# Attention with a mixture of experts on one core: the first two token tiles of an expert as one pair, and the order of the second layers

## The chip, the cores and the metric

The kernel runs on one core of one Trainium2 chip. The metric is the device time of the whole program in microseconds, lower is better. A time is the median of several runs. Besides the runs there is one profiled execution, from which all rows below come.

Names of the engines in the rows: PE is TensorE (matmuls), PEld its loads of the stationary operand, DVE is VectorE, ACT is ScalarE, POOL is GpSimd, SP is SyncE. A q behind a name is that engine's instruction queue.

## The reference

The input is 2 x 1024 tokens of 512 values. They are normalized, and three things are added to the input: a causal attention (16 heads in 4 groups), a shared feed-forward layer, and a mixture of 32 experts of which each token uses six.

```python
def _route(xf, Wr, br):
    s = jax.nn.sigmoid(xf @ Wr.T + br)
    ...
    idx = jax.lax.top_k(masked, K)[1]          # K = 6 of E = 32
    ...
    return (idx, w * SCALE)
...
def step(acc, ew):
    w1, w2, g = ew
    h = jnp.square(jax.nn.relu(xf @ w1.T)) @ w2.T     # 512 -> 256 -> 512
    return (acc + g[:, None] * h, None)
...
shared = jnp.square(jax.nn.relu(hidden_tensor @ Ws1.T)) @ Ws2.T
return shared + moe_out
...
x = x + _L0_attn_ref(xn, ...) + _L0_ffn_ref(xn, ...)
```

## The kernel before

All products are of float32 values split into an upper part (fp32r) and a lower part (the rest), and made of three matmuls: upper x upper, upper x lower, lower x upper. ScalarE writes the upper part by a copy, VectorE the lower part by a subtraction.

Stages: normalizing, routing and the shared layer up to about 136 us; then the experts; then the attention, to the end. In routing VectorE makes the tables `tile_hot` (MAXT wide, line 1526) from which TensorE makes the list of tokens (line 761), and a transfer fills the padding of the expert outputs with zeros (`act.dma_start(y_d[MINT * P:, :])`, line 1183).

The experts' work is cut into tiles of 128 tokens. An expert has the tiles `lo` to `hi`, from a table that is computed in the run (`count_tiles`; at least two for each expert). With these inputs there are 111 tiles, 3 to 5 for an expert, and 20 of the 32 experts have 3. GpSimd gathers the token rows of a tile into one of four slots of `xg`. For each tile TensorE runs:

- `hidden_tile` (line 855): 12 matmuls of 256 columns with the tokens stationary and the first-layer weights moving, into `ps_h`; then four turns (transposes) of the next tile's tokens (`transpose_gathered`, line 849) into `ps_x`;
- `output_tile` of the tile before (line 878): 6 matmuls of 512 columns into `ps_y`;
- `transpose_hidden` (line 890): two turns of the squares `mhsq` into `ps_g`.

Around these ScalarE does `relu_hidden`, the upper part of the next tokens (`upper_tokens`), the copy of the output (`copy_output`) and the upper part of the turned squares (`upper_hidden`); VectorE squares (`square_hidden`) and does the lower parts (`lower_tokens`, `lower_hidden`). SyncE stores the copied output.

The weights of an expert (1 MB) are loaded into one of two buffers `eraw`, three experts ahead, by `store_tiles` (line 487) at the start of its round for an expert. They are split in four pieces: `upper_weights` on ScalarE, `lower_weights` on VectorE, two experts ahead. Pieces 0 and 1 stand in the work of the expert's first tile, 2 and 3 after its last tile.

The order on each engine is the order of the code in `expert_tiles` (TensorE), `expert_uppers` (ScalarE) and `expert_lowers` (VectorE); every engine runs its own queue in order and waits on semaphores. The four experts of a round are written out (`s` is 0 to 3), and the tiles after the first are a loop on each engine.

## Time and profile before

| | us |
|---|---|
| runs, median of 3 | 1525.64 (1524.73 to 1525.66) |
| profiled execution, its own time | 1526.73 |
| span of its core | 1525.0 |
| TensorE busy with matmuls | 1509.9 (99%) |
| TensorE busy with weight loads | 1302.1 (85%) |
| VectorE busy | 1132.8 (74%) |
| ScalarE busy | 837.9 (55%) |
| GpSimd busy | 298.3 (20%) |

The mean granted clock of TensorE is 0.999 of its full speed. Matmuls overlap in the pipeline, so that their durations are longer than their spacing: the busy time says that TensorE has work, and the chain that ended last gives the spacing. Of that chain 96% of the span is TensorE's, 2% VectorE's and 1% transfers.

### The profile page before, as it was taken

What the parts mean: (1) busy time and instruction counts of PE and PEld (TensorE: products, weight loads), DVE (VectorE), ACT (ScalarE), POOL (GpSimd) and SP (SyncE); (2) the same over time, 40 slices, a digit from 0 to 9 for tenths busy, and PEclk for the clock granted to TensorE, in tenths of its full rate; (3) what the DMA queues carried; (4) which work ended last, traced back from release to release, by engine and by line L of the source; (5) the groups of instructions that cost most, each with busy time, mean ns of one, the idle gap of its engine ahead of it and who ended that gap; (6) DMA issues with size and microseconds to landing.
All of it is one profiled execution on the core that took longest, in us unless ns stands there. A gap on an engine that the chain in (4) does not pass through costs nothing.

```text
span 1525.0 us, 31150 instructions
## 1 busy us (share of the span) xinstructions
PE 1509.9 (99%) x8552; PEld 1302.1 (85%) x8553; DVE 1132.8 (74%) x2586; ACT 837.9 (55%) x1753; POOL 298.3 (20%) x540
## 2 busy tenths in 40 slices
PE   9998999999999999999999999999999999999998
PEld 8877998899899888888888888888888888888886
DVE  7896666666666669859949948967975994994896
ACT  5574666666666635535625635644553553553553
POOL 0003344334344311011002002102102101200211
PEclk9999999999999999999999999999999999999999
DMA  8874777777876612102102103422211210210111
GB/s 318 301 302 165 218 243 233 229 234 228 258 234 207 228 35 70 43 21 76 55 7 79 45 28 120 149 62 85 67 34 41 69 41 21 76 34 28 56 42 55
DMA packets 64774, 184.34 MB, mean 121 GB/s; under 512 B 7136, under 2 KB 7264, under 8 KB 60000
## 3 DMA queue, kind: packets, MB, share of 16 engines
q1 hardware_dynamic: 39888, 112.56, 21.1%
q0 software_dynamic: 16640, 54.54, 13.1%
q10 hardware_dynamic: 8208, 16.78, 2.8%
q8 instruction: 19, 0.31, 0.1%
q14 instruction: 19, 0.16, 0.0%
HBM read 123.29 MB, written 60.56 MB: 121 GB/s over the span
## 4 chain that ended last, share of the span: by engine, by line
PE 96%; DVE 2%; DMA 1%; issue 0%; ACT 0%; ACTq 0%; DVEq 0%; SPq 0%
PE bank L663 8%; PE bank L665 8%; PE bank L993 8%; PE bank L664 8%; PE ps_s L663 7%; PE ps_s L665 7%; PE ps_s L664 7%; PE ps_s L980 5%; PE ps_s L982 5%; PE ps_s L981 4%; PE ps_s L860 4%; PE ps_s L883 4%; PE ps_s L864 3%; PE ps_s L861 3%; PE ps_s L887 3%; PE ps_s L884 3%
## 5 line engine op out<-in xcount | busy, mean ns | idle before, releaser
L1322 ACT ACTIVATE probs<-probs,negmax 128x128 f32<-128x128 f32 (+7 forms) x256 | 197.4, 774 | 122.5 <-DVE negmax L1736 121.9
L1330 ACT ACTIVATE pT_hi<-bank 128x512 fp32r<-128x512 f32 x288 | 164.5, 595 | 143.4 <-PE bank L993 117.5
L1347 DVE TENSOR_TENSOR pT_lo<-bank,pT_hi 128x512 fp32r<-128x512 f32 x288 | 189.7, 684 | 41.0 <-ACT pT_hi L1330 40.0
L1736 DVE CUSTOM_DVE_ANT_0 probs<-ps_s,causal 128x128 f32<-128x128 f32 (+7 forms) x256 | 189.5, 753 | 17.1 <-PE ps_s L982 14.9
L427 POOL TENSOR_TENSOR settled<-ident 128x1 f32<-128x1 f32 x192 | 46.5, 242 | 788.7 <-DVE acc L1765 778.7
L993 PE MATMUL bank<-ident,probs 128*128 128x128 f32 x1152 | 157.0, 272 | 0.0
L993 PEld LDWEIGHTS bank<-ident,probs 128*128 128x128 f32 x1152 | 136.9, 141 | 19.8
L663 PE MATMUL ps_s<-xT_hi,wa_hi 128*128 128x512 f32 x384 | 152.7, 398 | 0.0
L665 PE MATMUL ps_s<-xT_hi,wa_lo 128*128 128x512 f32 x384 | 150.9, 393 | 0.0
L664 PE MATMUL ps_s<-xT_lo,wa_hi 128*128 128x512 f32 x384 | 150.2, 391 | 0.0
L1745 DVE TENSOR_SCALAR probs<-probs,rnorm 128x128 f32<-128x128 f32 (+7 forms) x256 | 133.4, 521 | 9.1
L980 PE MATMUL ps_s<-kT_hi,qT_hi 128*128 128x512 f32 (+5 forms) x384 | 134.0, 349 | 1.0 <-DVE qT_lo L1716 0.5
L982 PE MATMUL ps_s<-kT_hi,qT_lo 128*128 128x512 f32 (+5 forms) x384 | 131.2, 342 | 0.0
L981 PE MATMUL ps_s<-kT_lo,qT_hi 128*128 128x512 f32 (+5 forms) x384 | 130.9, 341 | 0.0
L663 PE MATMUL bank<-pT_hi,v_hi 128*128 128x512 f32 x288 | 123.6, 429 | 0.6 <-DVE cT_lo L1347 0.6
L623 POOL DMA_INDIRECT xg<-normed_tokens,comb_idx x112 | 111.8, 998 | 23.3 <-issue 18.1
L1347 DVE TENSOR_TENSOR hT_lo<-ps_s,hT_hi 128x256 fp32r<-128x256 f32 x111 | 47.2, 425 | 92.0 <-ACT hT_hi L1245 53.5
L665 PE MATMUL bank<-pT_hi,v_lo 128*128 128x512 f32 x288 | 113.5, 394 | 0.0
L1251 ACT ACTIVATE ysb<-ps_s 128x512 f32 x111 | 66.5, 599 | 84.9 <-PE ps_s L887 65.7
L664 PE MATMUL bank<-pT_lo,v_hi 128*128 128x512 f32 x288 | 112.7, 391 | 0.0
L652 POOL DMA_INDIRECT comb<-expert_outputs,comb_idx x96 | 105.2, 1096 | 19.6 <-issue 11.5
L663 PE MATMUL bank<-wa_hi,cT_hi 128*128 128x512 f32 x256 | 101.5, 396 | 1.4 <-DVE cT_lo L1347 1.4
(197 smaller groups left out, 3596.3 us busy)
## 6 DMA issues: line engine op xcount, KB each, us to landing
eraw<-we SPq DMA_DIRECT2D x37, 1024.0 KB
expert_outputs<-ysb SPq DMA_DIRECT2D x111, 256.0 KB
araw<-wa SPq DMA_DIRECT2D x37, 512.0 KB, 4.3
expert_outputs<-comb ACTq DMA_DIRECT2D x1, 16384.0 KB, 47.4
normed_tokens<-xn SPq DMA_DIRECT2D x4, 1024.0 KB, 10.0
out<-acc SPq DMA_DIRECT2D x16, 256.0 KB
acc<-x SPq DMA_DIRECT2D x2, 1024.0 KB, 13.8
turned_tokens<-xT_hi SPq DMA_DIRECT2D x2, 1024.0 KB, 7.6
```

The source lines that it names most:

```text
L663: pe.matmul(out_, lh, rh, start=(first and k == 0), stop=False)
L664: pe.matmul(out_, lh, rl, start=False, stop=False)
L665: mm = pe.matmul(out_, ll, rh, start=False, stop=(last and k == parts - 1))
L980: pe.matmul(o, q_h, kT_hi[:, ks], start=True, stop=False)
L981: pe.matmul(o, q_h, kT_lo[:, ks], start=False, stop=False)
L982: mm = pe.matmul(o, q_l, kT_hi[:, ks], start=False, stop=True)
L993: mm = pe.transpose(ps_t[blk % 2][:, h * P:(h + 1) * P], probs[:, i % 2, h, a * P:(a + 1) * P], ident[:, :])
L1322: act.activation(pr, pr, ACT.Exp, bias=negmax[:, i % 2, a:a + 1], scale=-1.0, accum_out=rowsum[:, i % 2, a:a + 1]).then_inc(exp_ready, 1)
L1330: act.activation(pT_hi[:, blk % RING, :], ps_t[blk % 2][:, :], ACT.Copy).then_inc(pt_hi_ready, 1)
L1347: dve.tensor_tensor(out_, whole, upper.bitcast(F32), ALU.subtract).then_inc(signal, 1)
L1736: dve.tensor_tensor_reduce(halves(probs[:, i % 2, a, 0:keys]), ps_s[:, s:s + parts, 0:keys // parts], halves(causal[:, SQ - keys:]), -1.0, ...
L1745: dve.tensor_scalar(pr, pr, rnorm[:, i % 2, a:a + 1], None, ALU.mult).then_inc(probs_ready, 1)
```

## The change

The change is in the experts' stage.

- `hidden_pair`: the first two tiles of each expert are one pair. The first-layer weights are stationary and 256 tokens move, so the hidden layer comes out turned, in two halves of 128 hidden values (`ps_p[0]`, `ps_p[1]`). Relu, Square, upper and lower part are made for each half (`relu_pair`, `upper_pair`, `square_pair`, `lower_pair`), without turns. ScalarE makes the upper part from the Relu with its own Square, VectorE squares for the lower part.
- `output_first`: the second layer of the pair's first tile goes half by half. The pair's second tile is done in the loop or ahead of the next pair.
- Tiles from the third on are done as before, in the loop, but the turns of their squares (`transpose_hidden`) now stand between the upper and the lower matmuls of the second layer of the tile before.
- The last tile's second layer stands whole ahead of the next expert's pair, in a bank of its own (`ps_y2`), and the turns of the next pair's second tile of tokens ahead of that (`ps_x2`).
- The four weight pieces stand one behind the other around the pair's steps; none is left for after the loop.
- Every expert gets at least three tiles (`LEAST`), and the bound MAXT goes from 160 to 177. With it the width of `tile_hot` and of the list matmuls grows, and the zero fill goes from 64 to 81 tiles.
- VectorE waits for `room_free` ahead of the attention's first maximum.

```diff
 MINT = T * TOPK // P
-MAXT = MINT + 2 * E
+LEAST = 3
+MAXT = max(LEAST * (E - n) + min(n * TILES, (T * TOPK + (P - 1) * n) // P) for n in range(E + 1))
...
+            def hidden_pair(lo, s):
+
+                w_hi, w_lo = w1(hi_slot(s)), w1(lo_slot(s))
+                both = lambda x, k: x[:, k, :, :].rearrange("p t n -> p (t n)")
+                for m in range(KM):
+                    ms = slice(m * P, (m + 1) * P)
+                    if m == 0:
+                        pe.wait_ge(mx_hi, lo + 2)
+                    for k in range(KD):
+                        pe.matmul(ps_p[m], w_hi[:, k, ms], both(xgT_hi, k), start=(k == 0), stop=False)
+                        pe.matmul(ps_p[m], w_lo[:, k, ms], both(xgT_hi, k), start=False, stop=False)
+                    if m == 0:
+                        pe.wait_ge(mx_lo, lo + 2)
+                    for k in range(KD):
+                        mm = pe.matmul(ps_p[m], w_hi[:, k, ms], both(xgT_lo, k), start=False, stop=(k == KD - 1))
+                    mm.then_inc(mh_ready, 1)
+
+            def output_first(lo, s):
+
+                w_hi, w_lo = w2(hi_slot(slot_of(s))), w2(lo_slot(slot_of(s)))
+                for m in range(KM):
+                    pe.wait_ge(mhhi_ready, past(lo + (m + 1)))
+                    pe.matmul(ps_y, hT_hi[:, s % 2, m, 0, :], w_hi[:, m, :], start=(m == 0), stop=False)
+                    pe.matmul(ps_y, hT_hi[:, s % 2, m, 0, :], w_lo[:, m, :], start=False, stop=False)
+                    pe.wait_ge(mhlo_ready, past(lo + (m + 1)))
+                    mm = pe.matmul(ps_y, hT_lo[:, s % 2, m, 0, :], w_hi[:, m, :], start=False, stop=(m == KM - 1))
+                mm.then_inc(my_ready, 1)
...
             def expert_tiles(e, s, lo, hi, es):
 
-                pe.wait_ge(ew_lo, (e + NSH) * WP + 2)
-                hidden_tile(lo, slot_of(s))
-                after = pair_bound(pe, e + 2)
+                turn_tokens(lo + 1, ps_x2)
                 if s:
-                    output_tile(lo - 1, slot_of(s - 1))
+                    output_upper(lo - 1, s - 1, ps_y2)
+                    output_lower(lo - 1, s - 1, ps_y2)
...
-                transpose_hidden(lo, (e + (NSH + 1)) * WP)
-                with pe.Fori(lo + 1, hi) as p:
+                after = pair_bound(pe, e + 2)
+                pe.wait_ge(ew_lo, (e + NSH) * WP + 2)
+                hidden_pair(lo, slot_of(s))
+                pe.sem_inc(mt_ready, 2)
+                turn_tokens(lo + 2, ps_x)
+                pe.wait_ge(ew_lo, (e + (NSH + 1)) * WP)
+                output_first(lo, s)
+                with pe.Fori(lo + 2, hi) as p:
                     hidden_tile(p, slot_of(s))
-                    output_tile(p - 1, slot_of(s))
+                    pe.wait_ge(y_copied, past(p - 1))
+                    output_upper(p - 1, s, ps_y)
                     transpose_hidden(p)
+                    output_lower(p - 1, s, ps_y)
                 return after
...
+            def upper_pair(lo, m, s):
+
+                act.wait_ge(mrelu_ready, past(lo + (m + 1)))
+                act.activation(hT_hi[:, s % 2, m, :, :].rearrange("p t n -> p (t n)"), prelu[:, m, :],
+                               ACT.Square).then_inc(mhhi_ready, 1)
...
             def expert_lowers(e, s, lo, hi, es):
                 slot = slot_of(s + 2)
-                square_hidden(lo)
-                lower_tokens(lo + 1)
+                if s:
+                    lower_tokens(lo + 1, 1)
...
                 lower_weights(e + 2, 0, slot)
-                lower_hidden(lo)
                 after = pair_bound(dve, e + 2)
                 lower_weights(e + 2, 1, slot)
-                with dve.Fori(lo + 1, hi) as p:
+                square_pair(lo, 0)
+                lower_pair(lo, 0, s)
+                lower_weights(e + 2, 2, slot)
+                square_pair(lo, 1)
+                lower_pair(lo, 1, s)
+                lower_tokens(lo + 2)
+                lower_weights(e + 2, 3, slot)
+                with dve.Fori(lo + 2, hi) as p:
                     square_hidden(p)
                     lower_tokens(p + 1)
-                    lower_hidden(p)
-                lower_weights(e + 2, 2, slot)
-                lower_weights(e + 2, 3, slot)
+                    lower_hidden(p, s)
```

On ScalarE, at an expert's start, the row read before from the third and fourth weight piece of the expert before (here `w_hi`) to the second piece of the next:

```order
L1235 ACTIVATE w_hi<-eraw 128x512 x2
L1239 REGISTER_ALU
L1241 ACTIVATE mrelu<-ps_s 128x256
L1229 REGISTER_ALU
L1230 ACTIVATE xgT_hi<-ps_s 128x512
L1234 ISA
L1235 ACTIVATE w_hi<-eraw 128x512
L1251 ISA
L1251 ACTIVATE ysb<-ps_s 128x512
L1245 ACTIVATE hT_hi<-ps_s 128x256
```

Now, from the second piece on (`prelu` is the pair's Relu, one half in each instruction):

```order
L1283 ACTIVATE w_hi<-eraw 128x512
L1295 ACTIVATE prelu<-bank 128x256
L1299 REGISTER_ALU
L1300 ACTIVATE hT_hi<-prelu 128x256
L1283 ACTIVATE w_hi<-eraw 128x512
L1295 ACTIVATE prelu<-bank 128x256
L1299 REGISTER_ALU
L1300 ACTIVATE hT_hi<-prelu 128x256
L1276 REGISTER_ALU
L1277 ACTIVATE xgT_hi<-ps_s 128x4x128
```

The third piece moved from behind the loop to between the two halves of the pair, and the copy of turned squares is gone for the pair.

On VectorE at the same place, before, with the first two pieces around the first tile's steps:

```order
L1653 TENSOR_TENSOR mhsq<-mrelu 128x256
L1347 TENSOR_TENSOR xgT_lo<-ps_s,xgT_hi 128x512
L1660 ISA
L1347 TENSOR_TENSOR w_lo<-eraw,w_hi 128x512
L1347 TENSOR_TENSOR hT_lo<-ps_s,hT_hi 128x256
```

and now, from the second piece on (`phsq` are the pair's squares):

```order
L1416 TENSOR_TENSOR w_lo<-eraw,w_hi 128x512
L1722 REGISTER_ALU
L1723 TENSOR_TENSOR phsq<-prelu 128x256
L1416 TENSOR_TENSOR hT_lo<-phsq,hT_hi 128x256
L1744 REGISTER_ALU
L1416 TENSOR_TENSOR w_lo<-eraw,w_hi 128x512
L1722 REGISTER_ALU
L1723 TENSOR_TENSOR phsq<-prelu 128x256
L1416 TENSOR_TENSOR hT_lo<-phsq,hT_hi 128x256
L1416 TENSOR_TENSOR xgT_lo<-ps_s,xgT_hi 128x4x128
```

The third piece's lower part moved to ahead of the second half's square.

On TensorE, in the loop over an expert's later tiles, before:

```order
L883 MATMUL ps_s<-wa_hi,hT_hi 128x512
L884 MATMUL ps_s<-wa_lo,hT_hi 128x512
L887 MATMUL ps_s<-wa_hi,hT_lo 128x512 x2
L891 REGISTER_ALU
L896 MATMUL ps_s<-ident,mhsq 128x128 x2
```

and now:

```order
L920 MATMUL ps_s<-wa_hi,hT_hi 128x512
L921 MATMUL ps_s<-wa_lo,hT_hi 128x512
L932 REGISTER_ALU
L934 MATMUL ps_s<-ident,mhsq 128x128 x2
L928 MATMUL ps_s<-wa_hi,hT_lo 128x512 x2
```

The two lower matmuls moved from ahead of the turns of the squares to behind them.

## Rows read from the trace of the kernel before

**Rows 1.** Chain that ended last, within one tile: start, us, what, count

```profile
306.18 0.12 PE ps_s L861
306.77 0.44 PE ps_s L852 x4
307.21 0.23 PE ps_s L883
308.60 0.22 PE ps_s L896 x2
```

**Rows 2.** Busy us by stage: window, PE, PEld, DVE, ACT, POOL, clock, DMA, GB/s

```profile
84.00:121.00 37.00, 36.37 (x221) 28.28 (x219) 36.24 (x147) 31.05 (x74) 0.00 (x0) 1.00 0.65 246
135.80:142.80 7.00, 4.46 (x35) 3.90 (x33) 4.63 (x8) 1.67 (x5) 2.28 (x3) 1.00 0.74 270
142.80:534.50 391.70, 389.63 (x2631) 349.07 (x2632) 242.60 (x459) 263.52 (x569) 155.96 (x320) 1.00 0.73 232
```

**Rows 3.** Waits of the expert stage: total us, times, longest

```profile
PEld ps_s L896 <- DVE mhsq L1653: 5.3, 23, 0.3
```

**Rows 4.** Timeline of the stage's start: start, us, engine, instruction, [idle before]

```profile
140.09 0.44 PE L896 MATMUL ps_s<-ident,mhsq 128*128 128x128 f32 x2 [2.27 <-DVE mhsq L1653]
...
142.19 0.63 ACT L1235 ACTIVATE w_hi<-eraw 128x512 fp32r<-128x512 f32 x1 [3.73 <-DMA eraw<-we]
...
145.58 0.38 PE L860 MATMUL ps_s<-wa_hi,xgT_hi 128*128 128x256 f32 x1
```

**Rows 5.** Timeline around an expert's first tile

```profile
306.61 0.60 PE L852 MATMUL ps_s<-ident,xg 128*128 128x128 f32 x4
306.81 0.38 ACT L1241 ACTIVATE mrelu<-ps_s 128x256 f32<-128x256 f32 x1 [0.64 <-PE ps_s L864]
...
307.23 0.42 DVE L1653 TENSOR_TENSOR mhsq<-mrelu 128x256 f32<-128x256 f32 x1 [0.59 <-ACT mrelu L1241]
...
310.20 1.29 DVE L1347 TENSOR_TENSOR w_lo<-eraw,w_hi 128x512 fp32r<-128x512 f32 x2
...
311.96 0.38 PE L896 MATMUL ps_s<-ident,mhsq 128*128 128x128 f32 x2
...
312.20 0.38 PE L860 MATMUL ps_s<-w_hi,xgT_hi 128*128 128x256 f32 x1
```

**Rows 6.** One weight load, its later waits (160 to 530 us), output copies

```profile
356.36 0.35 SPq L490 DMA_DIRECT2D eraw<-we  x1
...
364.65 0.63 ACT L1235 ACTIVATE wa_hi<-eraw 128x512 fp32r<-128x512 f32 x1 [0.22 <-DMA eraw<-we]
...
  DMA eraw<-we: 1.4, 3
...
L1251 ACT ACTIVATE ysb<-ps_s 128x512 f32 x111 | 66.5, 599 | 84.9 <-PE ps_s L887 65.7 <-issue 11.8 <-SPq L498 7.4
```

**Rows 7.** Groups by shape: busy us, mean ns, idle before; and one timeline row

```profile
L1526 DVE TENSOR_SCALAR tile_hot<-lane,xf,tok_f 128x160 f16<-128x160 f16 x96 | 23.3, 313 | 0.0
L1524 DVE TENSOR_SCALAR row_hot<-lane,xf 128x128 f16<-128x128 f16 x48 | 8.5, 244 | 0.8 <-PE bank L761 0.8
L1347 DVE TENSOR_TENSOR w_lo<-eraw,w_hi 128x512 fp32r<-128x512 f32 x72 | 48.3, 691 | 10.7 <-ACT w_hi L1235 8.6 <-issue 0.5
L1347 DVE TENSOR_TENSOR hT_lo<-ps_s,hT_hi 128x256 fp32r<-128x256 f32 x111 | 47.2, 425 | 92.0 <-ACT hT_hi L1245 53.5 <-issue 36.6
...
120.58 0.59 PE L761 MATMUL bank<-tile_hot,row_hot 128*128 128x160 f16 x6 [0.62 <-DVE tile_hot L1526]
```

**Rows 8.** The zero fill (us to landing), and ScalarE's timeline before the experts

```profile
expert_outputs<-comb ACTq DMA_DIRECT2D x1, 16384.0 KB, 47.4
...
125.11 2.18 ACT L1235 ACTIVATE wa_hi<-eraw 128x512 fp32r<-128x512 f32 x4
133.20 0.60 ACT L1230 ACTIVATE xgT_hi<-ps_s 128x512 fp32r<-128x512 f32 x1 [5.90 <-PE ps_s L852]
```

**Rows 9.** Busy us and clock of one stretch, columns as in rows 2

```profile
53.70:57.10 3.40, 3.40 (x10) 2.73 (x10) 2.81 (x6) 2.54 (x5) 0.00 (x0) 0.50 0.99 395
```

More of the change, by code:

```diff
@@ L265, in moe_attention_kernel @@
         ps_y = ps_s[:, 3, :]
+        ps_x2 = banks[0][:, :]
+        ps_p = [bank[:, 0:2 * P] for bank in banks[1::2]]
+        ps_y2 = banks[2][:, :]
         consts_in = sem("consts_in")
```

140 lines of the change are left out of this document (88 added, 52 removed).

## The prediction

> **What bounds the kernel now.** I read, in this order, the busy time by stage, the chain that ended last inside one tile, the list of waits, and then the timelines of the places that the change touches. The expert stage runs from 135.8 to 534.5 us, 398.7 us, in two windows [rows 2]. In the long one TensorE is busy for 389.6 of 391.7 us at the full clock, while VectorE and ScalarE have about a third of their time free. The chain inside a tile is TensorE from end to end [rows 1]: 0.12 us for each of the 12 first-layer matmuls (256 columns), 0.44 for the four turns of the next tile's tokens, 0.23 for each of the six second-layer matmuls (512 columns), 0.22 for the two turns of the squares. That is 3.48 us, with the rounding of the 0.12. The 111 tiles make 386.3 us, so 12.4 us of the stage are idle. About 4.2 of them are at its start: 9.8 us pass from 135.80 to the third tile's first matmul at 145.58, with 5.6 us of TensorE work in them [rows 4]. TensorE's weight loads waited for the squares 23 times, 5.3 us in all [rows 3]; with what the restart costs I put 0.2 us on each of 31 experts, 6.2. The end takes 0.9 and single events 1.1. So only two things pay: less TensorE work, or fewer of these waits.
>
> **What the pair removes.** The first two tiles of an expert now give their hidden layer already turned (weights stationary, 256 tokens moving). Count and width of the matmuls stay: 24 of 256 columns for two tiles, 0.12 us each. No trace row has this orientation with these tiles; the nearest is the same width with weights as the moving side [rows 1], and I take it. The 2 x 32 = 64 paired tiles lose their turns of squares: 64 x 0.22 = **14.1 us off**, work 372.2 us. The tiles stay 111, since by the inputs each expert needs 3 to 5 (20 need 3), so the new minimum of three adds none. ScalarE gets four instructions of 128x256 for four before, VectorE the same; neither is near its limit.
>
> **What each pair waits for instead.** Count from T, the end of the pair's last first-layer matmul. TensorE turns the next tokens (0.44), does the three second-layer matmuls of the first half (0.70), two of the second half (0.46), and wants the second half's lower part at T+1.60. The way there: ScalarE starts its Relu 0.20 after the matmuls end from 306.61 to 306.81, [rows 5] and is done at T+0.58. VectorE is then still on the third weight piece: ScalarE's Relu of the first half (T-1.22), its Square (0.42, an estimate between the Relu's 0.38 and a 512-wide piece's 0.63; done T-0.35) and that piece (done T+0.15) come first, VectorE starts the piece's lower part at T+0.19 and is free 0.60 later, at T+0.79 (two pieces take 1.29 [rows 5]). Square to T+1.21, subtraction to T+1.66 (0.42 each), 0.09 to TensorE: T+1.75 to 1.77, so a wait of about 0.17. A restart costs too: at 311.96 the two turns started late and the next matmul came 0.24 later instead of some 0.13 [rows 5]. I take **0.30 us for each of 31 pairs, 9.3**, where before 6.2 were lost. The bounds: zero (then the layout is slack throughout) and 0.5. The upper part of the second half is due at T+1.14 and ready at about T+1.12, so there is nothing in hand there either, but its delay would only eat the other.
>
> **The last tiles.** Turns of squares inside the second layer: TensorE asks for them 0.94 us after the token turns instead of 1.40. The earliest squares are ready at 307.65, and TensorE, with its token turns done at about 307.05, would ask at 307.99 [rows 5]. 0.3 us in hand: nothing. The third weight pieces no longer stand ahead of these squares, so the old 0.2 per expert goes. The last tile's second layer ahead of the next pair needs the copy of the turned squares 0.2 + 0.38 us after the turn; 0.46 of lower matmuls and 0.44 of token turns cover it. At the very end no token turns cover, so 0.3 us stays of 0.9.
>
> **The start.** The first pair needs tile 1 turned (135.80 to 136.24) and copied (137.05): 0.9 idle. Its hidden layer ends at 139.95, the token turns at 140.4. ScalarE's queue holds two weight pieces ahead of the pair's first Relu, and they wait for the transfer that lands at 142.19 [rows 4]. Two pieces at 0.52, Relu 0.38, Square 0.42 and the hand-over give 144.2: 3.8 idle. Three more waits (0.4, 0.2, 0.5) follow, since everything is late together. The third tile's first layer starts at 146.7, against 145.58. Idle time 5.8 instead of 4.2, with 0.44 less work.
>
> **Larger tables.** The bound on tiles goes from 160 to 177. VectorE is busy for 36.2 of 37 us in the routing stage [rows 2], and TensorE's last list matmuls wait for it at 120.58 [rows 7], so a longer queue there shows one to one. 96 instructions get 17 elements more. Nothing shows their slope; between 0 and 1.04 ns an element (the 512- and 256-wide subtractions, 691 and 425 ns [rows 7]) it is 0 to 1.7 us, of which VectorE's earlier waits take some. I take **0.5**. The 177 columns cost TensorE 7 ns in each of 96 matmuls, 0.7 us, which fit into its own wait. The zero fill grows from 64 to 81 tiles: 47.4 us [rows 8] become 60, it ends near 115 instead of 103 and slows the store of the residual. ScalarE waits for that before the first expert's weights, with 5.9 us idle behind these [rows 8]; without this cover it would cost up to 5.5. VectorE's new wait ahead of the attention's first maximum is for stores issued over 20 us before: nothing.
>
> **The sum.** 372.2 + 5.8 + 9.3 + 0.3 + 1.1 = 388.7 us against 398.7: 10.0 off. With 0.5 in routing, 9.5 off. The profiled execution took 1526.7 us, of which its span is 1525.0; it would become 1517.2. The median of the runs is 1.1 us lower, 1525.64, and so the forecast is **1516.1**. Uncertainty of the restarts and hand-overs makes it 1511 to 1520.5.
>
> **Rival 1, the weights come late, and it ends slower.** A load of 1 MB landed 8.29 us after its issue (356.36 to 364.65), and ScalarE waited for three of them, 1.4 us in all [rows 6]. In the new order load, first piece (0.52: four took 2.18 [rows 8]), output copy (0.60 [rows 6]) and two issues of the SyncE queue (0.35 each) form a loop of about 1.9 us plus the landing, 10.0 to 10.2 us, against a three-tile body of 10.2. With little in hand, landings of 8.7 cost about 5 us over the 20 three-tile bodies, and from 9.1 the whole gain is gone; 9.4 would give 1529. For: the body gets shorter with the same bytes, and three loads were late before. Against: the copies stand further from the load now (4.7 us instead of 3.5), and the loads that were waited for, the slowest, took no more than 8.3. Chance 0.12, a third of it slower than before.
>
> **Rival 2, the routing table's instructions lose their speed.** 128 elements in 16 bits with one scalar operand took 244 ns, less than the 291 that 159 + 1.04 x 128 would give, so they run at more than one element a step; 160 with two scalar operands took 313 [rows 7]. If these too are fast now and an odd 177 breaks it, each gains about 0.14 us (177 x 1.04 less a quarter of it). All 96: 13.4, less 0.8 of slack, 1528.7, slower. Every second one, whose row starts at an odd multiple of 354 bytes: 6.7, 1522.5. Chances 0.03 and 0.05.
> The Trainium skill ("VectorE: DVE Perf Modes", section "Mode 2×_1P — pack two bf16 into one 32-bit read") asks for a 4-byte aligned operand, which half of the new rows are not; by it the time would be the 1522.5 just worked out. Its microarchitecture page ("Vector Engine (DVE) Microarchitecture Reference", section "Performance modes — why throughput varies by op and dtype") says that chips showed no effect of alignment and that an odd count is fine if both sides have it. No row here tells the two apart.
>
> **Rival 3, the clock.** 3.8 us of idle at the start are longer than any gap before. At 53.7 to 57.1 us the granted clock was 0.50, the lower of the two levels, 1.2 GHz [rows 9], right after TensorE had run 3.8 us of 32-column matmuls. A like stretch here would lose at most half of 3.4 us of work, 1.7: 1517.8, inside the forecast's range, chance 0.1 of it.
> The Trainium skill ("TensorE: Matmul & The Clock Gate", section "HAM oscillation — how this bites in real kernels") says that waits between bursts of matmuls send the clock back to its lower level; by it this rival would hold. The gap of 2.27 us in the old start [rows 4] ran at the full clock [rows 2].
>
> **Rival 4, the pair's waits are other than laid out.** None: 19 us off, 1507, chance 0.09. 0.5 each: 1522, chance 0.08. **That it doesn't do what it says**, as with a dearer matmul in the new orientation (0.01 us more each makes 7.7 us for 768), I give 0.03.
>
> **How the numbers follow.** Forecast 0.60, rival 1 0.12, rival 2 0.08, rival 4 0.17, the last 0.03. The range of 8 in 10 goes from 1508.5 to 1522.5; it leaves out the worse half of rival 1, all of the dearest case of rival 2 and half of the fastest case. The boundary of 0.2%, about what a measurement of this kernel can tell from no change, is at 1522.6 and 1528.7: faster 0.84, same 0.10, slower 0.06.
>
> **What would show it.** Turns of squares should be 94, for 222. A three-tile expert should take about 10.3 us for 10.65. TensorE should wait at the second half of the pair's second layer for VectorE, some 0.2 to 0.3 us, 31 times; not there: rival 4. ScalarE's waits for weight transfers should be few; 20 of them with half a microsecond: rival 1. The list instruction should take 315 to 330 ns; 450: rival 2. The third tile's first layer should start about 1.1 us later after the stage's start. The forecast is wrong if a paired matmul is spaced at more than 0.12 us.

## The result and the profile after

The changed kernel is slower: 1533.67 us (median of 4 runs, 1531.73 to 1535.34) against 1525.18 (4 runs, 1523.57 to 1525.66), a ratio of 1.0057 with a 95% interval of 1.004 to 1.0074. The forecast was 1516.1 with a range up to 1522.5, so both the sign and the range were wrong. The profiled execution took 1532.91 us, its span 1531.1. The runs below were timed in four sets, in which the kernel before took 1524.43 to 1525.60 us; so two changed kernels are best compared by their distance from the kernel before, or by the length of the stage in their traces.

Busy microseconds by stretch in the kernel after (window, then PE, PEld, DVE, ACT, POOL with their counts, granted clock, DMA share, GB/s): routing, the start of the expert stage, the rest of it, and the 5.3 us behind the start's long wait:

```profile
84.00:121.00 37.00, 36.53 (x217) 28.59 (x216) 36.31 (x146) 30.76 (x74) 0.00 (x0) 1.00 1.03 388
135.96:147.57 11.61, 7.06 (x39) 5.60 (x38) 8.40 (x15) 6.32 (x13) 2.91 (x6) 0.80 0.86 324
147.57:543.24 395.67, 385.06 (x2500) 329.74 (x2498) 239.44 (x453) 277.45 (x562) 161.57 (x317) 1.00 0.69 225
...
144.70:150.00 5.30, 5.30 (x19) 4.28 (x20) 3.31 (x7) 2.65 (x6) 0.00 (x0) 0.52 0.69 282
```

Against [rows 2]: routing is the same. The expert stage runs from 135.96 to 543.24, 407.3 us, where it took 398.7. In its long stretch TensorE is now without work for 10.6 us (395.67 less 385.06); before it was for 2.1. What TensorE's weight loads waited for in the experts' stage of the kernel after, from 150 to 540 us (total us, times, longest):

```profile
PEld ps_s L899 <- DVE hT_lo L1416: 20.1, 36, 0.9
PEld bank L858 <- issue: 17.3, 31, 1.1
```

[rows 3] had one wait of 5.3 us there. A load runs ahead of its matmul, so these sums are larger than TensorE's loss. I therefore measure the loss from the starts of matmuls, phase by phase, over the 31 experts behind the first:

| phase | least time | mean after | lost, 31 experts | forecast |
|---|---|---|---|---|
| pair's first layer, 24 matmuls | 2.87 | 2.87 | 0 | 0 |
| second layer of the pair's first tile | 1.47 | 2.00 | 16.5 | 9.3 |
| last tile's two lower matmuls, up to the next tokens' turns | 0.55 | 0.84 | 9.2 | 0 |
| these turns | 0.36 | 0.41 | 1.6 | 0 |
| start of the stage, with what its clock cost | | | 7.4 | 5.8 |
| end and single waits | | | 0.4 | 1.4 |

Work of 372.2 us and 35.1 us lost make the 407.3. (The least times are those of the same matmuls in the loop: 1.47 for six of 512 columns, from the start of the first to the start of what follows.)

### The profile page after: what moved, and what is told of

It is laid out like the page before. It is cut to its first block, busy times and chain, and to the rows that moved or that the text cites. A ratio compares the mean times of both kernels' runs of the same rounds, so it can differ in the third digit from the quotient of the medians.

```text
span 1531.1 us, 30937 instructions
## 1 busy us (share of the span) xinstructions
PE 1504.8 (98%) x8424; PEld 1283.9 (84%) x8425; DVE 1132.5 (74%) x2586; ACT 854.1 (56%) x1753; POOL 304.1 (20%) x540
## 3 DMA queue, kind: packets, MB, share of 16 engines
q0 software_dynamic: 16640, 54.54, 12.5%
## 4 chain that ended last, share of the span: by engine, by line
PE 85%; DVE 8%; issue 2%; ACT 2%; DMA 1%; ACTq 1%; DVEq 0%; SPq 0%
PE bank L669 8%; PE bank L671 8%; PE bank L1040 8%; PE bank L670 8%; PE ps_s L669 6%; PE ps_s L671 6%; PE ps_s L670 6%; PE ps_s L1027 5%; PE ps_s L1029 4%; PE ps_s L1028 4%; PE ps_s L908 1%; PE ps_s L911 1%; PE ps_s L907 1%; PE ps_s L928 1%; PE ps_s L920 1%
## 5 line engine op out<-in xcount | busy, mean ns | idle before, releaser
L629 POOL DMA_INDIRECT xg<-normed_tokens,comb_idx x112 | 118.4, 1057 | 23.8 <-issue 19.2
L671 PE MATMUL bank<-wa_hi,cT_lo 128*128 128x512 f32 x256 | 100.0, 391 | 0.0
L670 PE MATMUL bank<-wa_lo,cT_hi 128*128 128x512 f32 x256 | 99.7, 389 | 0.0
## 6 DMA issues: line engine op xcount, KB each, us to landing
expert_outputs<-comb ACTq DMA_DIRECT2D x1, 20736.0 KB, 61.8
normed_tokens<-xn SPq DMA_DIRECT2D x4, 1024.0 KB, 10.6
```

The lines of the kernel that those rows point to most:

```text
L670: pe.matmul(out_, lh, rl, start=False, stop=False)
L671: mm = pe.matmul(out_, ll, rh, start=False, stop=(last and k == parts - 1))
```

## The pair's second layer

In the trace of the kernel after, around the pair of one expert (start, us, engine, instruction, [idle before]); T is 399.33, the end of the pair's first layer:

```profile
397.46 0.63 ACT L1283 ACTIVATE w_hi<-eraw 128x512 fp32r<-128x512 f32 x1
398.12 0.69 DVE L1416 TENSOR_TENSOR w_lo<-eraw,w_hi 128x512 fp32r<-128x512 f32 x1 [0.92 <-ACT w_hi L1283]
398.73 0.42 DVE L1723 TENSOR_TENSOR phsq<-prelu 128x256 f32<-128x256 f32 x1
399.25 0.42 DVE L1416 TENSOR_TENSOR hT_lo<-phsq,hT_hi 128x256 fp32r<-128x256 f32 x1
399.33 0.60 PE L858 MATMUL ps_s<-ident,xg 128*128 128x128 f32 x4
399.53 0.38 ACT L1295 ACTIVATE prelu<-bank 128x256 f32<-128x256 f32 x1
399.60 0.68 DVE L1416 TENSOR_TENSOR w_lo<-eraw,w_hi 128x512 fp32r<-128x512 f32 x1
400.20 0.42 DVE L1723 TENSOR_TENSOR phsq<-prelu 128x256 f32<-128x256 f32 x1
400.72 0.42 DVE L1416 TENSOR_TENSOR hT_lo<-phsq,hT_hi 128x256 fp32r<-128x256 f32 x1
401.20 0.50 PE L899 MATMUL ps_s<-wa_hi,hT_lo 128*128 128x512 f32 x1
...
386.20 0.63 ACT L1283 ACTIVATE wa_hi<-eraw 128x512 fp32r<-128x512 f32 x1 [0.50 <-issue]
```

VectorE has no gap from 398.12 to 401.1: second weight piece, square, lower part, third piece, square, lower part. The forecast let it wait for ScalarE's third piece; here that piece had long been there (VectorE took it at T+0.27, ScalarE had made it by T+0.12), and what came ahead of it on VectorE was late. The chain begins at ScalarE's second piece. The last row, from another expert, shows what that one waits for: 0.50 us of "issue", for which the timeline names nothing. Between the copy of the output and this piece stands ScalarE's load of a register with the next expert's bound (`pair_bound`, line 393). Such instructions are in no busy time, but the profile lists them by source line (instruction, count, shortest/median/longest ns, first and last start). Here they are for this piece, and for all experts from 150 to 540 us:

```profile
L393 ACTq TENSOR_LOAD <-first_pair x1: 722/722/722, 385.2 to 385.2; - x1
...
L393 ACTq TENSOR_LOAD <-first_pair x31: 274/347/760, 157.9 to 533.3; - x31
```

The piece starts 1.10 us behind the copy's start there, and in all 31 experts it starts 0.36 to 0.40 us later than the load alone lasts: 0.65 us behind the copy for a load of 0.27, 1.14 for one of 0.76. Why the load lasts longer in some experts is not shown. Two edits take these links apart.

**e2_third_late.** VectorE's third piece behind both halves:

```diff
-                lower_weights(e + 2, 2, slot)
                 square_pair(lo, 1)
                 lower_pair(lo, 1, s)
                 lower_tokens(lo + 2)
+                lower_weights(e + 2, 2, slot)
                 lower_weights(e + 2, 3, slot)
```

> The changed kernel with VectorE's part of the third weight piece behind the second half of the pair and the lower part of the next tokens; ScalarE's order stays. Theory A (VectorE's queue is what the second half's lower matmuls wait for): the second layer of the pair's first tile, 2.00 us on average for 1.47 of work, takes 1.50 to 1.60, so 31 times 0.45 less, 14 us: 1520. Theory B (ScalarE's Relu and Square, or the hand-overs, set it, and VectorE is only the last link): it stays at 1.85 or more, 1531 to 1534.

Measured: 1520.85 us against 1524.43 of the kernel before, ratio 0.9973 (0.9962 to 0.9985). The phase takes 1.63 on average (1.60 to 1.79). The same place in its trace, with T at 391.62:

```profile
392.23 0.43 DVE L1723 TENSOR_TENSOR phsq<-prelu 128x256 f32<-128x256 f32 x1 [0.25 <-ACT prelu L1295]
392.76 0.42 DVE L1416 TENSOR_TENSOR hT_lo<-phsq,hT_hi 128x256 fp32r<-128x256 f32 x1
393.27 0.47 PE L899 MATMUL ps_s<-wa_hi,hT_lo 128*128 128x512 f32 x1
```

The square now waits for the Relu and not for VectorE, and the lower matmul starts at T+1.65, where the order alone would have it at T+1.60. Theory A holds, with a little less than it expected: 31 x 0.374 = 11.6 us, 11.5 in the length of the stage (395.7 for 407.3), and 12.1 in the times against the kernel before.

**e5_loads_first.** Both register loads at the expert's start, ScalarE's shown:

```diff
+                after = pair_bound(act, e + 2)
...
-                after = pair_bound(act, e + 2)
                 upper_weights(1, slot, arrived)
```

> The changed kernel with one edit: ScalarE and VectorE load the register with the next expert's bound at the start of an expert and not between the first and second weight piece. In the run on the start order both edits stood together, and the second layer of the pair's first tile took 1.74 us there for 2.00. Theory A (the load of the register delays ScalarE's second weight piece by 0.17 to 0.6 us, and VectorE's whole chain of second piece, square, lower part, third piece, square, lower part hangs on it without slack): here too 1.74 to 1.76, 31 times 0.25 less, 8 us: 1525.5, and the start stays as it was (first matmul of the pair's second layer some 9 us after the stage's start). Theory B (it was the order of the first expert that shifted all later ones): it stays at 1.95 or more, 1533.

Measured: 1525.81 us against 1524.45, ratio 1.0007 (0.9998 to 1.0017), 7.9 us less than the changed kernel's 1533.67 (7.1 against the kernel before, 6.7 in the length of the stage). The phase takes 1.74 to 1.76 in 30 of 31 experts. In its trace, with T at 251.14:

```profile
248.61 0.60 ACT L1311 ACTIVATE ysb<-bank 128x512 f32 x1
249.10 0.62 ACT L1283 ACTIVATE w_hi<-eraw 128x512 fp32r<-128x512 f32 x1
249.75 0.69 DVE L1416 TENSOR_TENSOR w_lo<-eraw,w_hi 128x512 fp32r<-128x512 f32 x1 [0.33 <-ACT w_hi L1283]
...
251.29 0.69 DVE L1416 TENSOR_TENSOR w_lo<-eraw,w_hi 128x512 fp32r<-128x512 f32 x1
...
252.90 0.50 PE L899 MATMUL ps_s<-wa_hi,hT_lo 128*128 128x512 f32 x1
```

ScalarE's piece follows 0.49 behind the copy's start, where it was 0.65 at best and 1.10 in the row at 386.20. The lower matmul starts at T+1.76, which is the T+1.75 to 1.77 of the prediction. So the layout of the prediction was that of a kernel without the register load; the 0.16 to 0.65 us by which the load delayed the piece made 0.53 us of loss from 0.27. At its new place the load is short, 0.27 to 0.29 us on ScalarE in all 31 experts. The edit moved VectorE's load too; that ScalarE's is the one that counts is read from the trace of the kernel after, where VectorE waits for ScalarE's piece (0.92 us in the row at 398.12).

## The end of an expert

The 17.3 us of "issue" ahead of the token turns (L858) fell in no term of the forecast. Ordered by the slot (0 to 3) of the token rows that are turned next, the stretch from the lower matmuls to the turns was 0.55 to 0.64 us for slot 0, 0.66 to 0.80 for slots 1 and 2, 0.81 to 0.91 for slot 3; at the ends of rounds 1.07, 1.17, 1.25 and 1.32 to 1.37. The slots differ in one thing for TensorE, the path through the nested Ifs of `turn_tokens`.

**e1_nest_reversed.** The same nest, written the other way round:

```diff
-                with pe.If(q // 2 % 2 == 0):
-                    with pe.If(q % 2 == 0):
-                        transpose_gathered(0, q, bank)
+                with pe.If(q // 2 % 2 == 1):
+                    with pe.If(q % 2 == 1):
+                        transpose_gathered(3, q, bank)
...
```

> The changed kernel with the nested Ifs around the token turns written the other way round, so that slot 3 of the token rows comes first and slot 0 last; every slot still gets the same instructions. Theory A (TensorE waits for its own sequencer, which has to take branches with too little work queued ahead): the stretch from an expert's last two lower matmuls to the next expert's token turns, 0.57 to 0.63 us where the next slot is 0 and 0.81 to 0.91 where it is 3, turns round: about 0.60 for slot 3 and 0.85 for slot 0; at the ends of rounds, 1.07 for slot 0 and 1.32 to 1.37 for slot 3, likewise. The time stays within 2 us of 1533.7. Theory B (the gathered token rows come late): slot 3 stays the longest.

Measured: 1531.44 us (one run, 2.2 below the changed kernel's 1533.67; 1524.43 before). The lower matmuls and the turns behind them at two ends of an expert, the first with slot 0 next and the second with slot 3, in the kernel after:

```profile
209.04 0.71 PE L928 MATMUL ps_s<-wa_hi,hT_lo 128*128 128x512 f32 x2
209.59 0.64 PE L858 MATMUL bank<-ident,xg 128*128 128x128 f32 x4
...
219.96 0.71 PE L928 MATMUL ps_s<-wa_hi,hT_lo 128*128 128x512 f32 x2
220.81 0.65 PE L858 MATMUL bank<-ident,xg 128*128 128x128 f32 x4
```

and the same two in the kernel with the nest reversed:

```profile
207.85 0.71 PE L928 MATMUL ps_s<-wa_hi,hT_lo 128*128 128x512 f32 x2
208.65 0.65 PE L858 MATMUL bank<-ident,xg 128*128 128x128 f32 x4
...
218.76 0.71 PE L928 MATMUL ps_s<-wa_hi,hT_lo 128*128 128x512 f32 x2
219.38 0.65 PE L858 MATMUL bank<-ident,xg 128*128 128x128 f32 x4
```

0.55 and 0.85 us became 0.80 and 0.62: the cost goes with the place in the nest and not with the slot. At the ends of rounds slot 0 went from 1.07 to 1.37 and slot 3 from 1.32 to 1.37 down to 1.02 to 1.10. So TensorE waits for its own sequencer, which leaves the loop, adds to registers and takes branches while only two matmuls (0.46 us) are queued. The profile lists the branches by source line. In the kernel after, for the end with slot 0 next (lines 863 and 864) and for the one with slot 3 next (863 and 869):

```profile
L863 PEldq COMPARE_BRANCH  x1: 85/85/85, 209.1 to 209.1; - x1
L864 PEldq COMPARE_BRANCH  x1: 66/66/66, 209.3 to 209.3; - x1
...
L863 PEldq COMPARE_BRANCH  x1: 218/218/218, 220.0 to 220.0; - x1
L869 PEldq COMPARE_BRANCH  x1: 208/208/208, 220.4 to 220.4; - x1
```

At these ends a branch takes 0.07 to 0.09 us into the first arm and 0.20 to 0.24 into the other, so the two paths differ by 0.28 us, and the two stretches by 0.30. With the nest reversed the long branches are on the path of slot 0. At the end of a round the jump back and what it does with registers (line 417, 0.22 us each) come on top, 0.5 in the stretch:

```profile
L417 PEldq COMPARE_BRANCH  x8: 79/217/218, 194.6 to 540.8; - x8
```

Before the change the nest always stood behind twelve matmuls.

The Trainium skill ("Advanced Engine Details and Errata", section "Control Flow Timing") gives about 51 ns for an unconditional and 108 ns for a comparing branch; the comparing branches here took less on one path and twice that on the other.

**e3_last_written_out.** If that is the cause, the cure is to have no branch behind little work. The last tile is taken out of the loop on TensorE, ScalarE and VectorE; behind its hidden layer stand both turns, and its second layer follows at once:

```diff
+                with pe.If(hi > lo + 3):
+                    with pe.Fori(lo + 2, hi - 1) as p:
...
+                end = hi - 1
+                hidden_tile(end, slot_of(s))
+                if s < SLOTS - 1:
+                    turn_tokens(end + 2, ps_x2)
...
+                output_upper(end - 1, s, ps_y, end)
+                output_lower(end - 1, s, ps_y)
+                output_upper(end, s, ps_y2, half=0)
+                output_lower(end, s, ps_y2, 0)
```

> The changed kernel with the last tile of each expert written out behind the loop: its twelve first-layer matmuls stand ahead of both turns of tokens, the squares are turned in the middle of the second layer before, and the tile's own second layer follows at once, so that no branch of TensorE stands behind fewer than six matmuls. Theory A (branches of TensorE's own sequencer cost 0.30 us at the end of each expert, 0.5 more at the end of a round): these 9.4 us go, and 0.05 for each turn, 1.6. But ScalarE's second weight piece now waits for its own register load in half the experts, hidden in the others behind TensorE's delay, and would do so in all, so the second layer of the pair's first tile goes from 2.00 to about 2.2, 6 us back: 1529, between 1523 and 1531. Theory B (gathers or the hand-over of the turned squares set the end of the expert): 1533 or more, with the idle time named by another engine.

Measured: 1540.46 us, ratio 1.0105 (1.0088 to 1.0122). A miss by 11 us; the time is one that theory B would have given. The largest of TensorE's waits, 150 to 540 us:

```profile
PEld bank L883 <- ACT xgT_hi L1283: 21.9, 31, 1.1
```

The second nest was 0.19 us late on average (from the first turns to it 0.62 us, in e6 below 0.44), since it comes only four turns behind the first, and the pair's first matmul had a new wait, put down to ScalarE's tokens. The second layer of the pair's first tile did not go up to the 2.2 us that were expected; it took 1.74 to 1.81, since the pair itself now starts later and ScalarE's delay is hidden behind that.

**e6_one_nest.** Both turns in each arm of one nest, and the tokens' copy earlier on ScalarE and VectorE:

```diff
+                def both(slot):
+                    transpose_gathered(slot, q, ps_x)
+                    transpose_gathered((slot + 1) % XG, q + 1, ps_x2)
...
                 relu_hidden(hi - 1)
                 upper_tokens(hi)
+                if s < SLOTS - 1:
+                    upper_tokens(hi + 1, 1)
...
```

> The kernel with the last tile written out, where both turns of tokens now stand in one nest of Ifs (eight turns in each arm) and not in two behind each other, and ScalarE and VectorE do the second tile's tokens ahead of the copy of the output. In the run before, the second nest began 0.25 us late with four turns queued ahead of it, and the pair's first matmul waited for ScalarE's tokens 31 times. Theory A (TensorE's sequencer runs ahead by a few instructions only; a nest costs nothing behind twelve matmuls and its full time behind four or fewer): no gap around the turns, the pair's first matmul does not wait, and the excess at an expert's end, 0.35 us before, is under 0.1; the second layer of the pair's first tile at 1.75 to 2.0. 11 us for the ends and 4 for the pair: 1519, between 1515 and 1523. Theory B (a second limit of the same size stands at the expert's end, the copy of the turned squares or the output buffer): 1530 or more.

Measured: 1532.3 us, ratio 1.0044 (1.0029 to 1.006). Half a hit: the turns have no gap any more (0.79 us for two, whatever the slot, for 1.03 in e3), which is 7.4 of the 8.2 us against e3. The wait of the pair stayed as it was, under another name, now that ScalarE is done long before:

```profile
PEld bank L899 <- issue: 21.7, 31, 1.1
```

**e7_all_three** put the found parts together (e2, e5, e6 and the start, below):

> All found causes together: last tile written out with both turns in one nest, VectorE's third weight piece behind the pair's second half, the register loads at the expert's start, and for the first expert the pair's steps ahead of the third expert's weight pieces. Each theory's idle time is added: 31 times 0.14 in the pair's second layer, some 5 at the start, 0.5 at the end, 2 for single waits, with 372.2 us of work: the stage takes 384 us, and the time is 1511 (1508 to 1515), faster than both kernels. If the parts hide one another's gain (ScalarE or VectorE now sets the end of an expert), 1517 or more.

Measured: 1523.52 us, ratio 0.9997 (0.9988 to 1.0006). 12.5 us of the sum were missing, and the trace has them all in one place. The last second layer took 1.68 to 1.75 us (2.2 at ends of rounds) and the pair's first layer 2.97, 31 times the same, as already in e3 and e6:

```profile
307.64 0.42 DVE L1457 TENSOR_TENSOR hT_lo<-ps_s,hT_hi 128x256 fp32r<-128x256 f32 x1 [0.20 <-PE ps_s L947]
...
308.29 0.63 PE L947 MATMUL bank<-wa_hi,hT_lo 128*128 128x512 f32 x2
309.08 0.19 PEld L899 LDWEIGHTS bank<-xgT_hi,w_hi 128*128 128x128 f32 x1 [0.60 <-issue]
```

TensorE's queue sat at the wait for `hT_lo` until 308.1. From there to the pair's first load of weights at 309.08 are 0.97 us, with two matmuls (0.46) and TensorE's own load of the next expert's bound in them, the same that delayed ScalarE. Its instructions in this stretch:

```profile
L393 PEldq TENSOR_LOAD <-first_pair x1: 310/310/310, 308.2 to 308.2; - x1
L393 PEldq FUSED_REGOPS  x1: 162/162/162, 308.6 to 308.6; - x1
```

With an addition ahead and a check of the bound behind, the instructions of line 393 fill 308.11 to 308.82, and two register additions and the pair's waits the rest. In the changed kernel the same load stands at the same place and cost nothing (0.46 us from the last lower matmuls to the pair): there the four turns and the second layer, 1.9 us of work, stand ahead without a wait, and the sequencer was early (at one end of a round the load began at 196.19, the pair at 197.53).

The Trainium skill ("DMA: Bandwidth & Descriptors", section "Latency and other measured facts") lists a floor of about 600 ns for a `tensor_load`. The instruction of that name is shorter here, 0.31 us in the row above; it is with the other instructions of its source line that it comes to 0.7.

**e9_load_in_cover.** That load is moved to where TensorE waits for the turned squares anyway:

```diff
-                after = pair_bound(pe, e + 2)
                 pe.wait_ge(ew_lo, (e + NSH) * WP + 2)
                 hidden_pair(lo, slot_of(s))
...
                 output_lower(end - 1, s, ps_y)
+                after = pair_bound(pe, e + 2)
```

> The kernel with all three parts, and TensorE's register load of the next expert's bound moved from ahead of the pair to behind the lower matmuls of the tile before the last, where TensorE has to wait for the turned squares' copy anyway. In the run before, the expert's last second layer took 1.69 to 1.72 us for 1.47 of work (2.23 at round ends), and the pair's first layer 2.97 for 2.87. Theory A (the sequencer comes late from the wait for the last lower part, with two matmuls of 0.46 us queued for a register load of some 0.9 us): 1.47 and 2.87 inside a round, about 1.8 to 2.0 at a round's end; 31 times 0.32 less, 10 us: 1513. Theory B (the gap is the pair's own waits, for tokens, their lower part or the weights): it stays, 1523.

Measured: 1510.25 us, ratio 0.99 (0.9883 to 0.9918), 13.3 less than e7 (14.4 against the kernel before, 14.5 in the length of the stage). The waits in the same stretch:

```profile
PEld bank L899 <- issue: 2.4, 7, 0.4
```

The last second layer takes 1.36 to 1.47 us, at the ends of rounds too, the pair's first layer 2.87 in 24 experts and 2.97 in the seven that begin a round. Theory A holds, and the round's jump cost less than expected there (0.2 us with both phases).

**e10_early_lower.** VectorE's last lower part waits for the pair's second layer only:

```diff
-                lower_hidden(hi - 1, s, 0)
+                lower_hidden(hi - 1, s, 0, past(lo + 1))
```

> As the run before, and VectorE's lower part of the last tile's turned squares waits for the pair's first second layer only, not for that of the tile before, so that it ends some 0.4 us sooner and TensorE's sequencer has the whole second layer ahead of it at the jump of a round. Theory A: the last second layer at a round's end goes to 1.5 to 1.7 us, 2 us less in all: 1511, faster than the kernel before by 13 us. Theory B (the jump of 0.5 us is code that has to be brought in): it stays at 1.8 or more there, 1513.

Measured: 1508.49 us (1506.61 to 1509.69), ratio 0.9884 (0.9867 to 0.9901). The 2.97 at the start of a round are gone, and the stage is 0.6 us shorter in the trace; the ranges of this run and the last overlap, so that the part by itself is not shown in the time. The 2 us that were expected of it had been had in e9 already. The whole is 1.2% faster than the kernel before and 25 us faster than the changed one. Its stage takes 384.0 us, which is the 384 of the sum. ScalarE's waits for weight loads in it:

```profile
ACT w_hi L1308 <- DMA eraw<-we: 5.4, 6, 1.3
...
ACT wa_hi L1308 <- DMA eraw<-we: 4.4, 6, 1.1
```

Here rival 1 begins: ScalarE waited 12 times for a load, and four of 31 pairs took 1.98 to 2.10 us again. With a three-tile body of 10.15 us the loop of load, piece, copy and issue is the next limit, as the prediction had worked out.

## The start, and the clock

The first pair's second layer began at 144.68 instead of the 144.2 of the forecast. TensorE was idle for 3.86 us, and ran at the lower clock, 1.2 GHz, from there to 150.0 (the 0.52 of the table above): rows of matmuls of 512 columns stand 0.43 us apart.

```profile
144.68 0.76 PE L896 MATMUL ps_s<-wa_hi,hT_hi 128*128 128x512 f32 x1 [3.86 <-DVE w_lo L1416]
...
146.10 0.63 PE L896 MATMUL ps_s<-wa_hi,hT_hi 128*128 128x512 f32 x1
146.53 0.63 PE L897 MATMUL ps_s<-wa_lo,hT_hi 128*128 128x512 f32 x1
```

**e11_busy_wait.** Fifteen matmuls of 512 columns in the wait, for the first expert alone:

```diff
+                if s == 0:
+                    with pe.If(es == 0):
+                        for _ in range(15):
+                            pe.matmul(ps_x2, w1(hi_slot(slot_of(0)))[:, 0, 0:P], w2(hi_slot(slot_of(0)))[:, 0, :], start=True, stop=True)
```

> The changed kernel with fifteen matmuls of 512 columns added on TensorE, for the first expert alone, into a bank that nobody reads then, in the wait of 4.1 us ahead of the pair's second layer. Theory A (the low clock there comes of the idle time): the granted clock stays at full speed, the six matmuls of the pair's second layer are 0.23 apart and the third tile's first layer takes 1.43 us for 2.42, 2 us less than the changed kernel's 1533.7: about 1532. Theory B (the low clock has another cause, as the transfers or the stage's change of work): 0.43 apart and 2.4 us as before.

Measured: 1531.15 us (1529.78 to 1531.73), the same stretch at full clock:

```profile
144.70:150.00 5.30, 4.77 (x29) 3.69 (x28) 3.74 (x8) 3.25 (x7) 0.18 (x1) 1.00 0.69 278
```

So the idle time brought the clock down: theory A. From the pair's first matmul to that of the next pair 19.1 us passed, for 20.3: the clock cost 1.2 us, since the pair's second layer waits for VectorE at either clock. (The medians are 2.5 us apart; the trace gives the clock no more than the 1.2.) After 3.86 us idle the clock was low, after the waits of 1.45 and 1.44 us in e4 below and the 2.27 of [rows 4] it stayed at full speed. What the Trainium skill ("TensorE: Matmul & The Clock Gate", section "HAM oscillation — how this bites in real kernels") says of waits between bursts of matmuls, and the prediction had weighed, is borne out for the longest of them alone.

**e4_start_order.** For the first expert, pair before weight pieces:

```diff
+                after = pair_bound(act, e + 2)
+                def pair_uppers(first):
+                    if not first:
...
+                        upper_weights(1, slot, arrived)
                     relu_pair(lo, 0)
                     upper_pair(lo, 0, s)
+                    if not first:
+                        upper_weights(2, slot, arrived)
```

> The changed kernel where, for the first expert alone, ScalarE and VectorE do the pair's steps ahead of the four weight pieces of the third expert, whose load lands at 142.35 us. Theory A (the start's wait and the low clock after it come from that queue): the first matmul of the pair's second layer goes from 144.68 to about 141, the granted clock stays at full speed, and the third tile's first layer starts at about 143 instead of 147.57; 5 us less, 1528.5. Theory B (the low clock comes from the change of work and not from the wait): matmuls of 512 columns at 0.43 us spacing there all the same, 2.5 us of the gain stay away.

Measured: 1522.03 us (1520.7 to 1523.09), ratio 0.9984 (0.9974 to 0.9993), 11.6 less than the changed kernel, over twice the 5 that were expected. The third tile's first layer begins 8.0 us after the stage's start instead of 11.6, and the clock stays up. The other 8 us were no effect of the start: this edit had also moved the register loads, which e5 then did alone. That is how the load was found.

## Larger tables, and a gain in the attention

**e8_lists_of_160** put the bound back: `MAXT = MINT + 2 * E`.

> The changed kernel with the bound on the tiles put back to 160: list instructions of 160 instead of 177 elements and a fill of 64 tiles; enough for these inputs, not for all. Theory A (the larger tables cost nearly nothing): list instructions at 313 ns instead of 324, 1 us less in all, 1532.5. Theory B (the larger fill delays the first transfers of the experts' stage, and with them the start): the first weight load of the stage lands 2 us or more earlier than at 142.35, and the time is 3 us or more below 1533.7.

Measured: 1536.32 us (1534.4 to 1537.06), ratio 1.007 (1.0055 to 1.0085): slower than with 177, which neither theory had. The list instructions, after and in e8:

```profile
L1595 DVE TENSOR_SCALAR tile_hot<-lane,xf,tok_f 128x177 f16<-128x177 f16 x96 | 23.8, 324 | 0.0
```

```profile
L1595 DVE TENSOR_SCALAR tile_hot<-lane,xf,tok_f 128x160 f16<-128x160 f16 x96 | 23.3, 320 | 0.0
```

By the busy time of the group the tables cost 0.5 us in all (23.3 before, too [rows 7]). The mean of one is no sure measure of the width: it was 313 ns before, 320 in e8 and 339 in e12 below, all three 160 wide. The expert stage of e8 is that of the changed kernel (407.8 us). Two things differ. Its routing ended 1.0 us later, but with the same code up to there that end varied from 134.5 to 137.6 us over the kernels with 177. And the attention, from its first matmul to the end of the span, took 990.3 us, as in the kernel before (990.7), while the changed kernel took 987.9 and the others with 177 took 987.7 to 988.1. What differs is the projections' matmuls (groups from 600 to 1500 us: busy, mean ns; e8, with 398 ns as in the kernel before, and the changed kernel):

```profile
L669 PE MATMUL ps_s<-xT_hi,wa_hi 128*128 128x512 f32 x336 | 133.8, 398 | 0.0
```

```profile
L669 PE MATMUL ps_s<-xT_hi,wa_hi 128*128 128x512 f32 x336 | 132.6, 395 | 0.0
```

**e12_160_in_place** keeps the 160 of e8, but the arrays stand where the changed kernel has them. Against e8:

```diff
-        tok_idx = sb("tok_idx", [P, MAXT + 1], I32)
+        tok_idx = sb("tok_idx", [P, MAXT + 18], I32)
```

> The kernel with lists of 160 tiles again (enough for these inputs), with one allocation made 17 words longer: the list of tokens, so that every on-chip array allocated behind it stands where it stands in the changed kernel. With lists of 160 the attention took 990.3 us from its first matmul to the end of the span, as in the kernel before (990.7); in the changed kernel and all others with 177 it took 987.7 to 988.1, and it was the projections' matmuls that differed (398 and 393, 391 ns for 395 and 391, 390). Theory A (it is the place of the arrays in the on-chip memory): 987.9 here, and a time of 1533.7. Theory B (it is the size of the output buffer in the main memory, or of the fill): 990.3, 1536.3.

Measured: 1531.82 us (1530.26 to 1533.48), 4.5 less than e8 and 2 less than theory A had. The attention takes 987.8 us, and the row above has 395 again: 2.6 us of the difference. In the profiles the rest comes of a stage that began 2.9 us sooner and was 1.2 shorter, which is no effect of this edit as far as is known. So the time does not decide between the theories, but the attention does: where an array stands in the on-chip memory moved its 1152 matmuls by about 2 ns each. Why one place is better is not shown.

## Why the prediction was wrong, point by point

- **Removed turns**, 14.1 us: right. 47 tiles are left outside the pairs, with the 94 turns that were forecast, and the pair's matmuls are 0.12 apart: first layer 2.87 us for 24.
- **The pair's wait**, 9.3 us: the mechanism was right (VectorE's third piece ahead of the second half), its size was off by 7.2. The step that failed is "VectorE starts the piece's lower part at T+0.19": the layout began at ScalarE's Relu of the first half and left out the register load between copy and second piece. e5 restores the layout to 0.01 us; e2 shows what VectorE's piece cost. The load took 0.27 to 0.76 us on ScalarE. I had set the upper bound at 0.5 a pair; the mean was 0.53.
- **The last tiles**, "nothing": wrong by 10.8, the largest term. The step that failed is that term itself: I laid out engines' data, and counted for TensorE's own instructions between the loop and the turns no time at all. The order of instructions that I had before me showed the branches behind two matmuls, and no rival had them. Register operations and branches are in no busy time, but the profile before had their price, by source line, for the load and for the first branch of the nest:

```profile
L387 PEldq TENSOR_LOAD <-first_pair x34: 297/303/1011, 132.2 to 531.3; - x34
...
L867 PEldq COMPARE_BRANCH  x111: 73/216/377, 134.8 to 528.4; - x111
```

  The prediction used none of these rows. The waits of 5.3 us at the squares [rows 3], which I put down to the third weight pieces, may have held some of this already; that was not tried.
- **The start**, 5.8: measured 7.4 with the clock's share. The pair's second layer began 0.5 later than laid out, and rival 3 held: 1.2 us for the 1.7 that it was allowed.
- **Tables and fill**: right that they cost next to nothing. Rival 2 fell: 324 ns at an odd width of 177, where the loss of speed would have shown some 450, and no half of the rows stood out. That is what the Trainium skill says in "Vector Engine (DVE) Microarchitecture Reference" (section "Performance modes — why throughput varies by op and dtype"), against the alignment rule in "VectorE: DVE Perf Modes" (section "Mode 2×_1P — pack two bf16 into one 32-bit read"), which the prediction had set beside each other. The fill took 61.8 us and delayed nothing (ScalarE's idle time of 5.90 us ahead of the first tokens is unchanged).
- **Attention**: taken as unchanged; 2.8 us faster (987.9 for 990.7). The 534.5 at which the prediction ended the old stage is 0.2 us behind the attention's first matmul.
- **Rival 1** did not occur in the changed kernel: its only wait for a weight load was the one at the start. It occurs in e10, whose body has the length at which it was to begin.
- **Rival 4**, dearer waits, had the right direction and too low a ceiling.

In sum for the profiled execution: 18.6 us of the stage above the forecast (7.2 + 9.2 + 1.6 + 1.6 less 1.0 of smaller terms), 0.3 less in routing, 2.7 less behind the old stage's 534.5: 15.6 between the forecast span of 1515.5 and the measured 1531.1.

## What to carry to other kernels

Lay out an engine's own instruction stream beside the data: here a register load with its operations took 0.7 us on TensorE and a branch 0.07 or 0.22, and they are free only as long as work is queued behind which they can run, counted from the last semaphore at which the queue had to wait. So place register loads and nests of Ifs behind long runs of matmuls or where the engine waits anyway, and read a group of idle time named "issue" as such a place: ask the profile for that source line, where the loads and branches stand with their times. When the busy share is 99% and an edit removes work, the gain is decided by which short waits replace it: here 14 us of turns were paid for with 23 us of waits, and the same edit with its instructions in another order gave 17 us.

## What the runs showed of the hardware

- A register load from on-chip memory took 0.30 to 0.31 us on TensorE in the changed kernel, 0.7 with the register operations of its line (e7), and up to 0.92 where it stands in e9. On ScalarE it took 0.27 to 0.76 and delayed the next instruction by 0.16 to 0.65.
- A comparing branch of TensorE's took 0.07 to 0.09 us into an If's first arm and 0.20 to 0.24 into the other at these places, so one path through two nested Ifs is up to 0.3 us dearer than another; the jump back at the end of the unrolled round costs 0.5 us with its register operations.
- 1152 matmuls of 512 columns are about 2 ns of 230 each quicker or slower with the place of the arrays in the on-chip memory (e8, e12), 2.5 us of this kernel, more than many edits give.
- The start of the expert stage varies by 3.1 us between executions of kernels with the same code up to there (134.5 in e7, 137.6 in e5), so that a term of 0.5 us in routing can't be read from two profiles.
